# A one-layer attention kernel: the value matmuls of the second pass take another place among the scores

## The reference, cut to what matters

```python
qh = (q @ Wq.T + bq).reshape(B, Sq, N_HEAD, D_HEAD)        # Sq 128, 16 heads of 16
kh = (k @ Wk.T + bk).reshape(B, Sk, N_HEAD, D_HEAD)        # Sk 12544
vh = (v @ Wv.T + bv).reshape(B, Sk, N_HEAD, D_HEAD)
scores = jnp.einsum('bqhd,bkhd->bhqk', qh, kh) / np.sqrt(D_HEAD)
scores = jnp.where(attention_mask[:, None, :, :], NEG_FILL, scores)
probs = jax.nn.softmax(scores, axis=-1)
out = jnp.einsum('bhqk,bkhd->bqhd', probs, vh)
...
x = x + cross_attention(layernorm(x), context, context, mask)
x = x + self_attention(layernorm(x))                       # 128 tokens
x = x + ffn(layernorm(x))                                  # quantised, 256 to 768 to 256
```

## Time and profile before

| what | value |
|---|---|
| median of 3 runs | 475.36 us (474.81 to 475.63) |
| the profiled execution, its time / its span | 475.08 us / 473.4 us |
| TensorE matmul busy | 448.7 us, 95% of the span |
| TensorE weight loads busy | 353.3 us, 75% |
| ScalarE busy | 384.1 us, 81% |
| VectorE busy | 347.9 us, 73% |
| second pass, first score to last value matmul | 229.3 to 426.1 us |

### The profile page before, as it was taken

How to read it: one execution, slowest core, us unless ns; L and a number is a source line. 1 busy time by engine, 2 the same in 40 slices (tenths; PEclk the granted TensorE clock), 3 DMA queues, 4 the chain that set the end, 5 groups by cost and what they waited for, 6 DMA issues and landing times.

```text
span 473.4 us, 16042 instructions
## 1 busy us (share of the span) xinstructions
PE 448.7 (95%) x6464; PEld 353.3 (75%) x6464; DVE 347.9 (73%) x483; ACT 384.1 (81%) x436; POOL 100.2 (21%) x101
## 2 busy tenths in 40 slices
PE   7899999999999999996999999999999999999896
PEld 4776667766677676772698999999999999985463
DVE  5779999999999999999479988445555434605566
ACT  6688888888888888875698999999999999992433
POOL 1599533333333334306000000000000000000000
PEclk9999999999999999997999999999999999999999
DMA  7997656765557755948988698778789878100000
GB/s 252 345 384 264 223 207 246 296 247 214 213 212 295 285 216 209 363 188 287 422 316 289 242 329 295 272 264 297 259 287 331 279 276 268 70 3 1 1 2 15
DMA packets 33259, 112.01 MB, mean 237 GB/s; under 512 B 4048, under 2 KB 10576, under 8 KB 33232
## 3 DMA queue, kind: packets, MB, share of 16 engines
q1 hardware_dynamic: 29056, 105.07, 60.0%
q0 software_dynamic: 4032, 6.42, 4.7%
q10 hardware_dynamic: 144, 0.13, 0.1%
HBM read 74.44 MB, written 33.96 MB: 229 GB/s over the span
## 4 chain that ended last, share of the span: by engine, by line
PE 69%; DVE 11%; ACT 8%; issue 7%; SPq 2%; DMA 1%; POOL 0%; ACTq 0%; DVEq 0%; POOLq 0%
PE ps_a L1112 21%; PE ps_k L1126 20%; PE ps_a L967 10%; PE ps_k L958 10%; PE ps_a L1001 4%; ACT early L513 3%; DVE block_max L716 3%; DVE early L721 3%; ACT k_stack L466 1%; DMA ctx_b<-in_ctx 1%; DVE early L752 1%; ACT k_hi L497 1%; PE ps_a L1292 1%; PE ps_k L1309 1%; PE ps_a L1012 1%
## 5 line engine op out<-in xcount | busy, mean ns | idle before, releaser
L716 DVE TENSOR_REDUCE block_max<-ps_a 128x2 f32<-128x896 f32 x112 | 120.9, 1083 | 0.0
L1112 PEld LDWEIGHTS ps_a<-q_stack,k_stack 64*128 64x128 f32 x1568 | 96.3, 187 | 14.2 <-issue 12.5
L1112 PE MATMUL ps_a<-q_stack,k_stack 64*128 64x128 f32 x1568 | 105.5, 279 | 0.8 <-DVE q_stack L762 0.4
L513 ACT CAST early<-ps_a 128x896 bf16<-128x896 f32 x104 | 94.7, 910 | 6.1 <-PE ps_a L1001 6.1
L584 ACT ACTIVATE middle<-ps_a 128x1536 f32<-128x1536 f32 (+1 forms) x56 | 90.2, 1663 | 10.1 <-PE ps_a L1112 10.1
L584 ACT ACTIVATE early<-ps_a 128x1536 f32<-128x1536 f32 (+1 forms) x56 | 90.2, 1663 | 5.0 <-PE ps_a L1112 5.0
L967 PE MATMUL ps_a<-w_hi,k_stack 128*128 128x256 f32 x392 | 68.5, 297 | 0.0
L721 DVE TENSOR_TENSOR early<-early 128x896 bf16<-128x896 bf16 x104 | 65.6, 631 | 0.6
L958 PE MATMUL ps_k<-k_stack,w_hi 128*128 128x448 f32 x224 | 60.7, 391 | 2.7 <-issue 1.3
L967 PEld LDWEIGHTS ps_a<-w_hi,k_stack 128*128 128x128 f32 x392 | 53.0, 188 | 11.3 <-issue 11.2
L1001 PE MATMUL ps_a<-k_hi,q_pair 32*128 32x448 bf16 x448 | 42.7, 370 | 10.9 <-ACT early L513 8.7
(11 more groups left out here) (198 smaller groups left out, 495.9 us busy)
## 6 DMA issues: line engine op xcount, KB each, us to landing
k_stack<-k_hi_scratch SPq DMA_DIRECT2D x68, 448.0 KB, 5.2
v_scratch<-early SPq DMA_DIRECT2D x14, 952.0 KB, 5.2
v_in<-v_scratch SPq DMA_DIRECT2D x14, 952.0 KB, 5.3
k_hi_scratch<-k_hi SPq DMA_DIRECT2D x28, 448.0 KB, 2.5
k_lo_scratch<-k_lo SPq DMA_DIRECT2D x16, 448.0 KB, 3.2
k_stack<-k_lo_scratch SPq DMA_DIRECT2D x16, 448.0 KB, 5.2
ctx_b<-in_ctx SPq DMA_DIRECT2D x7, 896.0 KB, 6.8
early<-in_ctx SPq DMA_DIRECT2D x6, 896.0 KB, 7.0
```

Source lines behind the costliest of these rows:

```text
L513: nc.scalar.copy(staged[:, u % 2], pair_scores(u, 0)).then_inc(max_copied, 1)
L716: nc.vector.tensor_reduce(block_max[:, 2 * u:2 * u + 2, par], pair_scores(u, 1), AX.X, ALU.max).then_inc(max_taken, 1)
L1112: last = nc.tensor.matmul(ps_a[:, base + bank, at * Q:(at + 1) * Q], k_stack[half, b_par, a, t * P:(t + 1) * P], q_stack[half, a, ab, :], ...
```

## The change

The order of TensorE's instructions in the second pass is

    ... S_s(u+2) A_l(u-1) A_s(u) S_l(u+3) | S_s(u+4) A_l(u+1) A_s(u+2) S_l(u+5) | ...

Ahead of the loop now stand S_s(2), A_s(0) and S_l(3); the loop runs over u from 2, so its last pass reaches into the next double block; the end has A_l(u-1), A_s(u), A_l(u+1) in a row. Each unit waits for the same exponential as before. The tiles, the number of instructions, the buffers and all other engines' programs are the same.

```diff
@@ -1136,31 +1136,40 @@
                     if masked and m == 0:
                         pe.wait_ge(mask_t_in[par], (b - par) * 8 + 16)
 
+                def next_scores(i, w):
+
+                    pe.wait_ge(exp_done, i * (2 * UNITS) + w + 1)
+                    nxt = w + 2
+                    if nxt % UNITS == 0:
+                        if nxt == UNITS:
+                            pe.wait_ge(consts_set, 9)
+                        arrive(i * 2 + nxt // UNITS, nxt // UNITS % 2, 0)
+                    if nxt % UNITS == HU:
+                        arrive(i * 2 + nxt // UNITS, nxt // UNITS % 2, 1)
+                    score(nxt // UNITS % 2, nxt % UNITS, i * UNITS + nxt // 2 + 1)
+
+                def weighted(w):
+
+                    add_up(w // UNITS % 2, w % UNITS, w % SLOTS_P)
+
                 def two_blocks(i, final):
 
 
-                    for u in range(0, 2 * UNITS, 2):
+                    for u in range(2, 2 * UNITS + (0 if final else 2), 2):
                         ending = final and u == 2 * UNITS - 2
-                        for w in (u, u + 1):
-                            if not ending:
-                                pe.wait_ge(exp_done, i * (2 * UNITS) + w + 1)
-                                nxt = (w + 2) % (2 * UNITS)
-                                if nxt == 0:
-                                    arrive(i * 2 + 2, 0, 0)
-                                if nxt == HU:
-                                    arrive(i * 2, 0, 1)
-                                if nxt == UNITS:
-                                    pe.wait_ge(consts_set, 9)
-                                    arrive(i * 2 + 1, 1, 0)
-                                if nxt == UNITS + HU:
-                                    arrive(i * 2 + 1, 1, 1)
-                                score(nxt // UNITS, nxt % UNITS, i * UNITS + w // 2 + 2)
+                        if ending:
+                            pe.wait_ge(exp_done, i * (2 * UNITS) + u + 1)
+                        else:
+                            next_scores(i, u)
+                        weighted(u - 1)
                         if u % UNITS == 0:
-                            pe.wait_ge(v_back[u // UNITS], i * 16 + 16)
-                        for w in (u, u + 1):
-                            if ending:
-                                pe.wait_ge(exp_done, i * (2 * UNITS) + w + 1)
-                            add_up(w // UNITS, w % UNITS, w % SLOTS_P)
+                            pe.wait_ge(v_back[u // UNITS % 2], i * 16 + 16 + u // (2 * UNITS) * 16)
+                        weighted(u)
+                        if ending:
+                            pe.wait_ge(exp_done, i * (2 * UNITS) + u + 2)
+                            weighted(u + 1)
+                        else:
+                            next_scores(i, u + 1)
 
                 arrive(0, 0, 0)
                 for u in range(2):
@@ -1169,6 +1178,10 @@
                     score(0, u, 1)
                 for _ in range(WARM_PASS):
                     nc.tensor.matmul(attended, zeros_b[:, 0:P], zeros_b[:], start=False, stop=False, skip_group_check=True)
+                next_scores(0, 0)
+                pe.wait_ge(v_back[0], 16)
+                weighted(0)
+                next_scores(0, 1)
                 with pe.Fori(0, NB // 2 - 1) as i:
                     two_blocks(i, False)
                 two_blocks(NB // 2 - 1, True)
```

## The result

The changed kernel took 480.47 us (median of 4 runs, 476.56 to 482.47) beside 475.09 of the kernel before: ratio 1.0097, 95% interval 1.0054 to 1.0139. The forecast was 475.1 and no change, the range ended at 477.6. It is **slower**, and the prediction was wrong. The first ratio stands for 4.6 us; its interval overlaps those of the later two, and what it holds beyond their 1.8 us doesn't come back. (The ratios are recorded ones of undisturbed executions, so one can be smaller than the quotient of the medians beside it.)

A forecast was written before the change was run, and what follows sets the result against it. Bound: a mixed circle of ScalarE and TensorE over two pairs, 6.92 us, becoming 6.91; 28 x -0.01 = -0.3, start and end 0, so 475.36 - 0.3 = 475.1 us. Own range 474.0 to 476.3; 8 in 10: 472.4 to 477.6.

The forecast's parts named there:

- The circle of 3.22 + 0.04 + 3.66 over two pairs: Second pass: two exponentials, wait to first load of large scores, TensorE's stretch to next small exponential; 6.92 us sets the pace.
- TensorE's own cycle: Second pass: same matmuls and turns in the new order, 3.41 us a pair, 6.82 for two; nothing taken.
- ScalarE's gaps: Second pass: idle ahead of small exponentials would vanish and come back ahead of large ones, in sum as now.
- start and end: Both ends of the second pass: large exponentials keep their instants, so 0 at each.
- the waits moved past others: Second pass, waits for a block's values and keys and SyncE's waits: slack covers them, costed at nothing.
- the -0.3 us: Second pass: overlap from large to small exponential 0.12 instead of 0.105, giving 0.01 a circle over 28 circles.
- the gate: Wait ahead of small scores in the second pass: first load 0.04 and 0.05 us after a large exponential's end, taken.
- above, the whole loss of a long pair, 0.11, in every pair: Upper bound for the wait ahead of small scores; lower bound 0, or -0.04 a circle. Kept as a rival.
- The slower rival: First load of small scores: a closed wait in every pair, 27 x 0.11 = 3.0 us more, 478.4; chance 0.15.
- The faster rival: Second pass: TensorE never waits, long pairs become short, 27 x 0.11 = 3.0 us less, 472.4; chance 0.22.
- The stop of the earlier trace: Weight loads pause 0.87 us before 256.96, once in the pass, cause unknown; left as is, -0.8 kept for the range.

The follow-up runs named there:

- the later two: The changed kernel, unaltered, timed twice more with 12 runs each against the kernel before: ratios 1.0037 and 1.0038.
- the split: Large exponentials made two instructions, nothing gated earlier, on the kernel before: 477.05 us, ratio 1.0044. With large scores gated by halves, on the new order: 477.13 us, 1.0045.
- the early gate: Kernel before, order kept, large exponentials in two halves, next large scores waiting first for the first half only: 472.33 us, ratio 0.9922.
- waits_swapped: Changed kernel with the exponential's wait put last in next_scores, behind the waits for keys: 475.83 us, ratio 1.0010; timed again 476.35 us, 1.0010.
- again: Changed kernel unaltered, timed again beside the kernel before with a new profile: 477.19 us, ratio 1.0037.
- the swapped kernels: Changed kernel with the exponential's wait last, 475.83 us; the same with large exponentials in halves and large scores gated by halves, 477.13 us.

## Why the prediction was wrong, by its own steps

- **The circle of 3.22 + 0.04 + 3.66 over two pairs**: right, and the best thing in it. It told the direction of every edit to it, and the size nearly: the split added 0.065 for the 0.09 expected, in both orders, and the early gate took the pace to TensorE's own 6.82 (measured 6.81).
- **TensorE's own cycle, ScalarE's gaps, start and end, the waits moved past others**: as forecast. Gaps stand ahead of 128 x 2048 and none ahead of 128 x 1536; no pause for keys or values appeared in any trace. The overlap from large to small is 0.104, as that from small to large was, so the -0.3 us was not there.
- **The step that failed is the gate**, "a large exponential's end to the load took 0.04 and 0.05, which I take". Its size was taken from the gate of large scores, behind whose wait nothing stands. Ahead of the small scores of units 0 and 4 `arrive` puts a second wait. The prediction listed `arrive` under the waits that are moved past others and costed it by whether keys are late; it didn't ask what two waits in a row cost when the first one is closed. The instruction could be seen in the trace before, at a gate that stood open. It measured 0.122 to 0.139 us instead of 0.051 at 24 gates; that is the 1.8 us. The bound that was kept, "above, the whole loss of a long pair, 0.11, in every pair", would have covered it.
- **Why all of it counts.** The circle goes from a unit to the unit four on. Half a block is four units, so the small units 0 and 4 lie in the same circle: it met the slow gate each time round, while the circle through units 2 and 6 had slack (its scores started 0.109 us after the load before, no pause). 24 gates x 0.076 on average = 1.8 us.
- **The slower rival** named the place, the first load of the small scores, and was right about the side. Its mechanism, losses in every pair because loads can't be pulled ahead, is out: only every second pair got longer, and waits_swapped has the gate in the same place at no cost. The rule of the Trainium skill that stood beside it (TensorE: Matmul & The Clock Gate, the step on loading the stationary operand: weight loads are pulled ahead of running matmuls) doesn't show as a cost of the place here: 13.87 us a block in waits_swapped, 13.86 before.
- **The faster rival** was out for this change, but its figure of 3.0 us was reached by another edit, at 3.5.
- **Outside the pass** the prediction took the opening and the joint between the passes as fixed. They were not: 3.3 us of the first difference lay there. That is part of why the first figure fell beyond the range. The later two ratios on the 475.36 us of the forecast would give 477.1 and 477.2 us, just within it: the gate alone does not carry the time beyond the range, the gate and the opening together did. But 1.8 us is well above the 0.95 that the prediction took for no change, so the forecast of no change fails on the gate alone.

## What to carry to other kernels

Find the closed loop of waits that is longer than any one engine's work, and count each latency on it; idle time of both engines in every turn is its mark, and an instruction made longer on the "idle" engine tests it. Where an order of work is changed, look at each gate that is now closed when it is reached, and see to it that the wait that will be the last to open sits on the first instruction itself. Which place in the source does that depends on the other waits: here it was behind waits against a register's value, and ahead of waits against constants. The trace tells, by a sequencer instruction between the signal and the first load. Moving work round this loop in another order changed nothing; opening its gate for a part of the work did.

## What was not expected of the hardware

- **A closed wait that is not on the weight load itself costs 0.06 to 0.09 us.** Where the load carried the exponential's wait, it came 0.051 or 0.052 us after the end of the exponential in the median (two orders, large and small units, six kernels). Where a wait on a register's value was written behind it, a sequencer instruction took the closed wait, and the load came at 0.122 to 0.139 us. With constants it is the other way round: a constant's wait written behind was issued ahead and cost nothing (0.051 and 0.052), and waits against constants written ahead of it pushed the closed one into an instruction of its own (0.113 or 0.114, the last double block of the swapped kernels).
- **Stops 2.2 to 2.5 us after an instruction fetch.** The stop of the earlier trace rows, which the prediction left open, came back in most traces at other places: 17 of over 0.42 us from load to load in twelve traces, none in the changed kernel's first and in waits_swapped, and all between 239 and 266 us, where the loop is run for the first time. One of three in again (weight loads; and the row of the instruction queue in a window of 255.7 to 255.8 us):

```profile
258.13 0.52 PEld L1112 LDWEIGHTS ps_a<-q_stack,k_stack 64*128 64x128 f32 x7 [0.99 <-issue]
```

```profile
q8 instruction: 1, 0.02, 60.0%
```

A fetch of 16 KB starts at 255.76 and the stop ends at 258.13. All 17 stops end 2.20 to 2.50 us after such a fetch has started; other fetches there show no stop, such as the six from 240 to 265 us in the changed kernel's first trace. On the later turns of the loop there are hardly any fetches and no stops; while the last double block, which is program of its own, is fetched (from about 401 us on), there are no such stops either. It fits that TensorE waits in the first turn for its own program; no run took the fetch away, so it is not shown. It costs 0 to 2.9 us an execution (the pass took 200.7 us in again, 197.8 in the first trace of the same kernel).
- **The clock at the start of an execution.** In five of the ten traces of the experiments the clock was at 1.2 GHz for 3.4 us or more within the first 27 us, or for 10 instead of 7 us ahead of the second pass. With a mean clock below 0.992 the kernel before took 2.3, 1.2 and 2.2 us longer in the median, in the three sets of executions beside the experiments. For changes worth 0.4% of this kernel four runs are too few.
